# Attention loops that go by pairs of heads instead of single heads, on TensorE, VectorE and ScalarE

## What is computed

```python
x = L0(x, ctx)   # causal self-attention (16 heads of 32), cross-attention to ctx
                 # without a mask (16 heads of 16), gated MLP (two token types)
x = L1(x, ctx)   # cross-attention with a key mask (16 heads of 64), GELU MLP
x = L2(x, ctx)   # one-headed attention of x to ctx, gate, RMS norm
x = L3(x, ctx)   # as L1, other weights

# the attention in each of them, per batch and head
scores = q @ k.T * scale            # 112 x 112 (self) or 112 x 375 (ctx)
scores = where(mask, scores, -3.4e38)
p = softmax(scores)
out = p @ v
```

## Time and profile before

| | us |
|---|---|
| median of 3 runs | 2152.37 (2145.38 to 2153.7) |
| profiled execution, its own time | 2153.12 |
| span in its profile | 2151.3 |
| TensorE busy | 1999.6 |
| VectorE busy | 1179.8 |
| GpSimd busy | 887.9 |
| ScalarE busy | 852.6 |

### The profile page before, as it was taken

One profiled execution on the slowest core, in us unless ns is written; L12 is line 12 of the kernel. 1 busy time (PEld: TensorE's weight loads), 2 busy tenths in 40 slices (PEclk: granted clock), 3 DMA queues, 4 the chain that ended last, 5 costly groups with the idle time before them and its releaser, 6 DMA issues.

```text
span 2151.3 us, 35629 instructions
## 1 busy us (share of the span) xinstructions
PE 1999.6 (93%) x12588; PEld 1694.3 (79%) x12588; DVE 1179.8 (55%) x3046; ACT 852.6 (40%) x2198; POOL 887.9 (41%) x1037
## 2 busy tenths in 40 slices
PE   4999897988889999999999999998878999998998
PEld 3865586766679999888888887996547888887898
DVE  6778766566555245354666645422165666664422
ACT  2026525565422112125666633322234666661321
POOL 3340302114048899974121126881043121103785
PEclk9999698897789999999999999999999999999999
DMA  3110100001013333331000022332131000001232
GB/s 120 40 55 2 45 8 15 9 21 50 3 43 105 117 108 114 122 103 36 14 20 12 12 83 69 108 108 75 67 102 42 9 18 12 22 2 40 88 109 83
DMA packets 38191, 118.87 MB, mean 55 GB/s; under 512 B 6169, under 2 KB 10265, under 8 KB 38017
## 3 DMA queue, kind: packets, MB, share of 16 engines
q1 hardware_dynamic: 31408, 107.92, 16.2%
q10 hardware_dynamic: 6608, 8.68, 1.4%
HBM read 114.75 MB, written 1.84 MB: 54 GB/s over the span
## 4 chain that ended last, share of the span: by engine, by line
PE 81%; DVE 9%; POOL 5%; issue 2%; ACT 2%; DMA 1%; DVEq 0%; SPq 0%; ACTq 0%; POOLq 0%
PE psum L544 15%; PE psum L545 13%; PE psum L546 13%; PE psum L755 8%; PE psum L766 7%; PE psum L809 6%; PE psum L537 4%; PE psum L660 4%; PE psum L662 4%; PE psum L661 4%; POOL wl L1603 3%; DVE rstd L1196 1%; DVE xc L1211 1%; POOL wh L1595 1%; PE psum L823 1%
## 5 line engine op out<-in xcount | busy, mean ns | idle before, releaser
L1603 POOL TENSOR_TENSOR wl<-raw,wh 128x256 fp32r<-128x256 f32 x656 | 517.7, 821 | 13.7
L1595 POOL TENSOR_SCALAR wh<-raw 128x1024 fp32r<-128x1024 f32 x164 | 183.7, 1120 | 459.5 <-PE psum L546 205.2
L544 PE MATMUL psum<-nh,wh 128*128 128x448 f32 x904 | 347.2, 384 | 14.5 <-DVEq L1379 7.8
L545 PE MATMUL psum<-nl,wh 128*128 128x448 f32 x904 | 336.9, 373 | 0.0
L546 PE MATMUL psum<-nh,wl 128*128 128x448 f32 x904 | 336.0, 372 | 0.0
L988 ACT ACTIVATE probs_t<-masked_t,nmin 112x375 f32<-112x375 f32 (+1 forms) x384 | 207.2, 540 | 129.8 <-DVE nmin L1314 113.3
L766 PE MATMUL psum<-cst,probs_t 112*125 112x112 f32 (+1 forms) x1304 | 240.5, 291 | 16.3 <-DVE probs_t L1325 16.2
L766 PEld LDWEIGHTS psum<-cst,probs_t 112*125 112x125 f32 (+1 forms) x1304 | 196.3, 194 | 59.0 <-DVE probs_t L1325 25.4
L1325 DVE TENSOR_SCALAR probs_t<-probs_t,rinv 112x376 f32<-112x376 f32 (+1 forms) x520 | 218.0, 419 | 18.5
L1451 DVE TENSOR_TENSOR hid_l<-scr,hid_h 128x448 fp32r<-128x448 f32 x108 | 94.1, 871 | 229.0 <-ACT hid_h L1063 228.4
L1314 DVE CUSTOM_DVE_ANT_0 masked_t<-psum,maskf 112x375 f32<-112x375 f32 x256 | 139.3, 545 | 124.4 <-PE psum L755 123.9
(11 more groups left out here) (178 smaller groups left out, 3854.8 us busy)
## 6 DMA issues: line engine op xcount, KB each, us to landing
raw<-in_walls SPq DMA_DIRECT2D x183, 512.0 KB, 3.5
raw<-in_ctxF SPq DMA_DIRECT2D x24, 375.0 KB, 3.0
ctxb<-in_ctxF ACTq DMA_DIRECT2D x8, 375.0 KB, 3.8
ctxt<-in_ctxK ACTq DMA_DIRECT2D x8, 375.0 KB
x<-in_xT ACTq DMA_DIRECT2D x2, 896.0 KB, 11.6
outT<-x SPq DMA_DIRECT2D x2, 896.0 KB, 5.8
mask<-in_kmask ACTq DMA_DIRECT2D x16, 41.0 KB, 2.6
vself<-in_tt SPq DMA_DIRECT2D x1, 448.0 KB, 6.8
```

The source lines that it names most:

```text
L544: nc.tensor.matmul(out, ah, bh, start=(i == 0), stop=False)
L545: nc.tensor.matmul(out, ah, bl, start=False, stop=False)
L1595: nc.gpsimd.tensor_scalar(high, src, 1.0, 1.0, ALU.mult, ALU.mult).then_inc(split_h, 1)
L1603: last = nc.gpsimd.tensor_tensor(low[cut], src[cut], high[cut].bitcast(F32), ALU.subtract)
```

## The change

All four loops (PE, ACT, DVE and what `projected` lists) now go by pairs of heads, `a.pair` = 2 (1 for memory). In one step of the loop:

- DVE takes the minima of both heads first, then one reciprocal over two columns for the pair before, then the two scalings of that pair. The low part of a K tile is done in the step in which PE projects it, not a head later.
- cross0 takes the same instruction for the minimum as the masked attentions, with a mask of zeros (`maskf[:, 0, :]`), and writes the scores to `masked_t`. The exponential reads them there, and PE waits for `maxed` in cross0 too.
- PE does the scores of a pair, its projections, the transposes of both heads of the pair two steps back, and then the value sums if a quad is due. `LAG` now counts pairs.
- ACT does both exponentials of a pair, then the pair's projections, then the copies of the transposes of both heads.
- `NPROB` goes from 3 to 6 and `masked_t` from 2 to 4 buffers (`NMASK`). `masked_t` moves into the space of the scratch tile `xc`.
- In cross1 and cross3 the V units come two and one heads later (`first`, `second`); the first V unit is no longer done ahead of the loop.

```diff
-NPROB = 3
+NPROB = 6
+NMASK = 4
...
-            first = {att_c0: -4}.get(a, -1)
-            second = {att_c0: -1}.get(a, 1)
+            first = {att_c0: -4}.get(a, 1)
+            second = {att_c0: -1}.get(a, 2)
...
-                    pe.wait_ge(a.maxed if a.mask else a.exped, s)
+                    pe.wait_ge(a.maxed, s)
...
             def attention(a):
-                for s in range(a.steps + LAG + 2):
-                    if s < a.steps:
-                        if a is att_2 or s % 2 == 0:
-                            scores(a, s)
-                        for unit in projected(a, s):
-                            project(a, *unit)
-                        if a is att_self and s % 2 == 0 and s // NH + 1 < B:
-                            values(s // NH + 1, s % NH // 8, s % 8 // 2)
-                    if 0 <= s - LAG < a.steps:
-                        turn(a, s - LAG)
-                    w = s - LAG - 1
-                    if 0 <= w < a.steps and w % a.quad == a.quad - 1:
-                        weigh(a, w // a.quad)
+                pairs, wide = a.steps // a.pair, a.quad // a.pair
+                for n in range(pairs + LAG + 2):
+                    heads = range(a.pair * n, a.pair * n + a.pair)
+                    if n < pairs:
+                        scores(a, heads[0])
+                        for s in heads:
+                            for unit in projected(a, s):
+                                project(a, *unit)
+                            if a is att_self and s % 2 == 0 and s // NH + 1 < B:
+                                values(s // NH + 1, s % NH // 8, s % 8 // 2)
+                    if 0 <= n - LAG < pairs:
+                        for s in heads:
+                            turn(a, s - LAG * a.pair)
+                    w = n - LAG - 1
+                    if 0 <= w < pairs and w % wide == wide - 1:
+                        weigh(a, w // wide)
...
-                        src = masked_s[s % 2][:, 0:a.nk] if a.mask else s_bank(s)[:, 0:a.nk]
+                        src = s_bank(s)[:, 0:a.nk] if a is att_2 else masked_s[s % NMASK][:, 0:a.nk]
...
+                m = {"causal": causal, "keys": maskf[:, b % 2, :], None: maskf[:, 0, :]}[a.mask]
+                nc.vector.tensor_tensor_reduce(out=masked_s[s % NMASK][:, 0:a.nk], in0=s_bank(s)[:, 0:a.nk],
+                                               in1=m, scale=1.0, scalar=BIG, op0=ALU.add, op1=ALU.min,
+                                               accum_out=col).then_inc(a.maxed, 1)
...
+                pairs, wide = a.steps // a.pair, a.nk + a.nk % 2
+                for n in range(pairs + LAG + 3):
+                    if n < pairs:
+                        for s in range(a.pair * n, a.pair * n + a.pair):
+                            smallest(a, s)
+                    late = range(a.pair * (n - 1), a.pair * n) if 0 < n <= pairs else ()
+                    if late:
+                        own = slice(late[0] % NPROB, late[0] % NPROB + a.pair)
+                        dve.wait_ge(a.exped, late[-1] + 1)
+                        nc.vector.reciprocal(rinv[:, own], rsum[:, own]).then_inc(a.recip, 1)
+                        dve.wait_ge(a.recip, n)
+                    for r in late:
                         pr = probs[r % NPROB][:, 0:wide]
                         nc.vector.tensor_scalar(pr, pr, rinv[:, r % NPROB:r % NPROB + 1], None, ALU.mult)\
                             .then_inc(a.scaled, 1)
```

More of the change, by code:

```diff
@@ L181, in __init__ @@
         self.quad = min(4, nh)
+        self.pair = min(2, nh)
         self.turn_w = max(group, self.chunks) * S
@@ L295, in build @@
         vS = vself[0:S, :].rearrange("p (b d) -> p b d", b=B)
-        masked_s = [masked_t[:, i, :] for i in range(2)]
+        masked_s = [masked_t[:, i, :] for i in range(NMASK)]
         probs = [probs_t[:, i, :] for i in range(NPROB)]
@@ L981, in attention @@
             def attention(a):
-                for s in range(a.steps + LAG):
-                    if s < a.steps:
+                pairs = a.steps // a.pair
+                for n in range(pairs + LAG):
+                    heads = range(a.pair * n, a.pair * n + a.pair)
+                    for s in heads if n < pairs else ():
                         act.wait_ge(a.maxed, s + 1)
@@ L998, in attention @@
                             context(a, s + 2)
-                    t = s - LAG
-                    if t >= 0 and t % a.group == a.group - 1:
+                    for t in range(heads[0] - LAG * a.pair, heads[0] - LAG * a.pair + a.pair):
+                        if t < 0 or t % a.group < a.group - 1:
+                            continue
                         g = t // a.group
```

65 lines of the change are left out of this document (29 added, 36 removed).

## The result

The kernel after takes 2076.66 us (median of 4 runs, 2071.08 to 2082.91), the one before 2153.03 in the same job; the ratio is 0.965, 95% interval 0.961 to 0.9691. The forecast was 2103 us with a range from 2082: the direction was right, the size 26 us short. The profiled execution takes 2073.76 us of its own time, with a span of 2072.0 us.

A forecast was written before the change was run, and what follows sets the result against it. PE, busy in 93% of the span, was taken as the bound, so only its waits or lower-clock time could return. 2153.12 - 42.5 (cross0) - 7 (self) = 2103.6, less 0.75: 2103 us, range 2082 to 2132.

The forecast's parts named there:

- The loop: In cross0, scores to next scores through two minima in a row: 1.87 us, where it was 3.49.
- cross0, 209.5 predicted: The cross0 stage up to the next stage: 193.5 us without clock losses plus 16, 42.5 less than 252.
- 6 + 5 + 3.5 + 5: PE's idling in cross0, in us: bare pairs 6, output instructions 5, scalings lengthened by GpSimd 3.5, filling and draining 5.
- 174 + 16: PE's busy time in cross0: 174 us of work at the upper clock level plus 16 us lost to the clock.
- four of the nine half-clock stretches stay: In cross0, stretches at the lower clock stay at start, end and two batch boundaries, 4 us each: 16 us.
- The rule that I weighed against the trace: Brief, frequent idling between matmul groups swings PE's clock between levels; by it all nine stretches in cross0 would stay.
- self, 120 predicted: The self stage: 127 us falls by 7 (bounds 2 and 18), 6 from idling and 1 from the clock.
- 6 of the 10 us of idling: In self, waits for the minimum and most for the scaling go, 6 of PE's 10 us idle; the rest is drain.
- I take 1: In self, 1 us of the 18 us clock loss comes back, since most lies in the last batch.
- The order changes, not the work: In cross1 and cross3 PE has no waits to lose, so the change gives 0 (bounds -4 and +6 us each).
- The slower rival: In cross1 and cross3 VectorE, waiting for K's high part, reaches the next minima late: 2180 us, chance 0.07.
- the second rival: In cross0 late scalings raise the transposes' waits from 8.5 to some 30 us, stretches staying: 2138 us, chance 0.08.

The follow-up runs named there:

- e4: The kernel after, with the second minimum of a pair in cross0 behind the reciprocal and the first scaling: 2123.67 us, 0.9854.
- e13: e4 with cross0's projections also spread, so that every pair has value sums or a projection: 2082.24 us, 0.9701.
- e1: The kernel before, with cross0 alone taking exponentials from SBUF behind a zero-mask minimum, PE's scores waiting for the minimum, heads single: 2126.57 us, 0.985.
- e16: The kernel before, with only the three numbers that spread the projections of cross0 changed: 2163.75 us, 1.0046.
- e3: The kernel after, with self by single heads again and the larger number of buffers kept: 2096.21 us, 0.9725.
- e12: The kernel after, with the value sums ahead of the transposes in all attentions: 2118.45 us, 0.9856.
- e11: The kernel after, with the second minimum behind reciprocal and first scaling in self, cross1 and cross3 instead of cross0: 2083.03 us, 0.9705.
- e7: The kernel after, with VectorE's low part of a key one pair later, behind the scalings, in all cross attentions: 2331.74 us, 1.0838.
- e10: The kernel after, with each head's transposes in cross1 and cross3 behind the projections of its own step, as before: 2079.04 us, 0.9691.
- e14: The kernel after, with the value sums of cross1 and cross3 straight behind the scores of the same step: 2117.03 us, 0.9812.
- e8: e4 with PE's transposes done twice in the bare pairs of cross0, 144 matmuls more: 2099.97 us, 0.9759.
- e15: The kernel after, with the value sums of cross1 and cross3 between K tile and V part of the same step: 2089.88 us, 0.9692.
- e5: The kernel after, with cross0's exponentials reading PSUM again and PE's scores waiting for them: 2113.96 us, 0.9799.

## Why the prediction was right in kind and 26 us short

**The loop** of 1.87 us: 1.88 measured. The waits of the scores for ScalarE are gone, as said; bare pairs idle 0.27 and 0.37 us where the timeline shows them, and 0.24 was worked out.

**cross0, 209.5 predicted, 201.5 measured.** The idle time was right as a sum: 19.5 us predicted (6 + 5 + 3.5 + 5), 19.0 measured (201.5 - 182.5). Its terms were not all: there is no wait for the scaling, which had 3.5, and there are 6.4 us of waits for ScalarE's copy, which had no term; that they cancel is luck. PE's busy time was put at 174 + 16 and is 182.5. The clock of 0.94 makes (1 - 0.94) x 201.5 = 12 us of loss instead of 16, and the work is some 3.5 us less than 174. The term that carried the uncertainty, "four of the nine half-clock stretches stay", was near by luck (in windows of 8 us the clock is low at the start, in three places between and at the end; the three between are shorter than the assumed 10 us): e4 and e13 show that the number of stretches goes by how bunched the idling is, which my step, a count by the share of busy time (92%), could not know. e4, with 0.52 us more in the loop, has a stretch in every batch again and 45 us more in the stage. The rule that I weighed against the trace (the Trainium skill, TensorE: Matmul & The Clock Gate, section A second HAM failure mode: psum-queue depth-cycling) would have left all the stretches; the trace agrees in e4, where brief idles come close together and each batch has its drop, and disagrees in e13, which idles as much and keeps 1.00 in all the windows shown.

**self, 120 predicted, 110 measured.** The term "6 of the 10 us of idling" holds: from first to last scores PE idles 9.4 us in e1 (115.7 - 106.3) and 2.5 after. Two things were missing. The granted clock of self in before's profiled execution (0.88) was lower than in the same code's other executions (0.96 in e1, 0.92 in e16), so that 5.6 of the 17 us are no gain of the change (e1, e3), and its 18 us of clock loss were no fixed property of the stage, which the step "I take 1" took them for. And PE's busy time fell by 4.8 us (106.3 to 101.5) with the same matmuls. With the time lost to the clock taken off ((1 - 0.96) x 115.7 and (1 - 0.94) x 104.0) it fell by some 6.4. The passages, 3 to 2 per four heads here too, would be 32 x 0.18 = 5.8. e12, which puts the third back, lost 4.8 us in self, but only 2.4 of them are busy time; the other 2.4 are waits. That the passages are self's busy time is argued, not shown.

**cross1 and cross3, 0 predicted, -5.9 and -5.8 measured.** This is the step that failed: "The order changes, not the work". The order is work, for PE pays for each passage to the small matmuls, and the new order has one fewer per four heads. My bound had a switch in it, from the earlier trace rows: -4 is 32 x 0.12, though the words beside it say half a switch, which would be 1.9. It was one whole switch per quad of 0.18, and it belonged in the sum. The rows needed for it stood in the prediction, three transposes in 0.39 us by themselves and 0.51 up to the value sums; I used them for cross0 and did not count them for these stages. The slower rival's premise, VectorE late at the minima, did not come about: PE has no wait there, and e11 shows cover even for the longer order. What would have brought a loss is the low part a pair later (e7), a mechanism that the prediction did not price.

**The sum.** Against 2103.6 for the profiled execution, 2073.76 is 29.8 less: self 10, cross0 8, cross1 and cross3 11.7. The median of the runs lies 2.9 us above the profiled one. The lower end of the range, 2082, took one stretch and self at its upper bound but left out the -4 of each of cross1 and cross3; it also took 9 us for self, where 18 - 7 is 11. With both it would have been 2072, and the measured time inside. The 2138 us of the second rival has no working beside it; the waits that it names came to nothing.

**Left open.** Why e1, with e4's loop, keeps 0.89 in its profiled execution where e4 has 0.78; by the other three executions of e1 the gap is smaller. Of e1's windows of 6 us, those with 4.82 and 4.63 us busy at 366 and 444 us were followed by no drop, those with 4.62 and 4.63 at 390 and 414 us were, and e4 has one of 4.49 at 522 us without a drop. In the kernel after, the same two waits (0.42 to 0.44 us for the minimum, then 0.50 for the copy) stand at the start of five batches: at 351 and 446 us the clock fell, at 376, 399 and 423 us it didn't. So bunching is shown as what loses the clock between e4 and e13, but no rule from which a drop could be foretold. And why cross0 of the unchanged code had 199.6 us in e10 and 199.5 in e14 while the others had 192.1 to 194.7.

## What to carry to other kernels

Where a step of a loop has more work than another, hand the movable work (here projections) to the poor steps before shortening anything else, but see first that the loop is shorter than the filled step: the same three numbers gave 12 us after the change and cost 7 before it. On PE count the passages from full-row to small matmuls per round of the loop, as one counts instructions, and put small next to small. When an instruction that frees a shared bank is moved behind others, follow the bank to its next writer: one pair later was 255 us. And before a stage is read from one profiled execution, compare its time with those of the others: e1's was 18 us below them.

## What the runs showed of the hardware

Evenly spread idles of PE, 10% of the time, left the granted clock at 1.00; the same 10% bunched once per batch took it to 0.50 in each batch (e13 and e4, 43.27 and 43.09 of 48 us busy). 144 useless matmuls made a stage 24 us faster (e8, 237.9 to 214.0 us). Passing from full-row matmuls to those on 64 rows or columns of the array costs PE 0.12 to 0.26 us at full clock, 0.18 on average; the way back from value sums costs no more than going on (e10, e12, e15). The same code's stage varies between profiled executions by 6 to 8 us, and its clock with it (self 115.7, 117.4 and 121.3 us at 0.96, 0.92 and 0.88; cross0 192.1 to 199.6 at 0.95 to 0.91), and whole executions of one kernel by up to 24 us (e5). So a stage with clock losses needs more than one profile before a term is drawn from it.
